# A perceiver layer: x loaded four groups ahead, stage 3 in another order, the gate's product in three fp32r products

## What is computed

```python
x = x + xattn(layernorm(x), ctx)     # cross attention to the 257 context rows, then [hc, hq, hc*hq, hc*bar] @ W_qv + b
x = x + attn(layernorm(x))           # z = layernorm(x); xg = z * sigmoid(z @ Wg.T + bg)
                                     # s = s @ A + xg * Bp; y = s . Cp + Dp * xg, over 32 tokens; layernorm(y + xg) * gamma + beta
x = x + ffn(layernorm(x))            # h = x @ tern(w_fc).T + low rank; relu(h)**2 @ tern(w_proj).T
```

## Time and profile before

| | |
|---|---|
| median of 3 runs | 589.56 us (588.4 to 592.37) |
| the profiled execution | 591.37 us, its span 589.6 us |
| PE busy | 501.3 us (85% of the span) |
| DVE busy | 428.4 us (73%) |
| ACT busy | 363.6 us (62%) |
| POOL busy | 334.3 us (57%) |
| granted clock of TensorE, mean | 0.95 |
| DMA | 69.9 MB, 41.5% of 16 engines' span |

### The profile page before, as it was taken

How to read it: one execution, slowest core, us unless ns; L and a number is a source line. 1 busy time by engine, 2 the same in 40 slices (tenths; PEclk the granted TensorE clock), 3 DMA queues, 4 the chain that set the end, 5 groups by cost and what they waited for, 6 DMA issues and landing times. The chain is left out here.

```text
span 589.6 us, 12951 instructions
## 1 busy us (share of the span) xinstructions
PE 501.3 (85%) x4070; PEld 420.2 (71%) x4070; DVE 428.4 (73%) x1197; ACT 363.6 (62%) x857; POOL 334.3 (57%) x424
## 2 busy tenths in 40 slices
PE   3596999999999999999998716975888988988995
PEld 2375777878787877877786506964777877877884
DVE  2589888888888878887887606943688788788643
ACT  3464767776767766776776405563846846846652
POOL 1488666675757575766665300002767767767653
PEclk9799999999999999999999957995989989989998
DMA  7543365545645475646565761546002202201102
GB/s 225 147 157 100 104 210 156 177 142 175 189 143 176 139 213 131 190 124 205 145 186 149 193 62 39 139 109 148 31 1 72 71 2 73 71 1 36 38 1 71
DMA packets 90035, 69.90 MB, mean 119 GB/s; under 512 B 49504, under 2 KB 73328, under 8 KB 89968
## 3 DMA queue, kind: packets, MB, share of 16 engines
q1 hardware_dynamic: 89968, 69.08, 41.5%
HBM read 55.96 MB, written 13.11 MB: 117 GB/s over the span
## 5 line engine op out<-in xcount | busy, mean ns | idle before, releaser
L1526 POOL TENSOR_TENSOR sq_lo<-scan_x,sq_hi 128x512 fp32r<-128x512 f32 x64 | 83.7, 1308 | 58.5 <-ACT sq_hi L1497 56.5
L1489 ACT ACTIVATE relu<-fc_ps,fc_square 128x512 f32<-128x512 f32 x64 | 43.9, 686 | 54.8 <-PE fc_ps L1438 54.8
L473 PE MATMUL turn_ps<-ident,ctxn 128*128 128x128 f32 x512 | 70.8, 283 | 4.3 <-DMA ctxn<-in_ctx 4.3
L1567 DVE SCALAR_TENSOR_TENSOR scan_x<-fc_ps,relu 128x512 f32<-128x512 f32 x64 | 44.0, 687 | 38.2 <-ACT relu L1489 37.5
L603 ACT COPY ctxT<-turn_ps 128x512 f32<-128x512 f32 x128 | 68.2, 581 | 5.2 <-PE turn_ps L473 5.1
L473 PEld LDWEIGHTS turn_ps<-ident,ctxn 128*128 128x128 f32 x512 | 58.6, 145 | 17.9 <-issue 13.2
L708 POOL TENSOR_TENSOR rstd<-ve,neg_half 128x1 f32<-128x1 f32 x64 | 35.3, 551 | 43.3 <-DVE ve L796 22.5
L722 POOL TENSOR_TENSOR hc_lo<-hc_probT,hc_hi 128x256 fp32r<-128x256 f32 x32 | 23.4, 730 | 56.3 <-ACT hc_hi L610 56.3
L1434 PE MATMUL fc_ps<-toeplitz,fc_T 128*128 128x512 f32 x128 | 54.1, 422 | 0.5 <-DVE scan_x L1567 0.5
L1434 PE MATMUL fc_ps<-xn_lo,fc_T 128*128 128x512 f32 x128 | 53.0, 414 | 0.0
L714 POOL TENSOR_TENSOR proj_in<-proj_in,fc_in 128x512 f32<-128x512 f32 x31 | 49.2, 1588 | 0.0
(11 more groups left out here) (188 smaller groups left out, 1413.3 us busy)
## 6 DMA issues: line engine op xcount, KB each, us to landing
ctxn<-in_ctx SPq DMA_DIRECT2D x32, 1024.0 KB, 5.3
resid<-in_x SPq DMA_DIRECT2D x32, 128.0 KB, 4.7
ctx_end<-in_ctx SPq DMA_DIRECT2D x32, 128.0 KB
gated_tokens<-gated SPq DMA_DIRECT2D x32, 128.0 KB, 5.0
out<-resid SPq DMA_DIRECT2D x8, 512.0 KB, 3.0
scan_x<-gated_tokens SPq DMA_DIRECT2D x60, 64.0 KB, 4.8
scan_tokens<-scan_x SPq DMA_DIRECT2D x4, 768.0 KB, 9.7
y_in<-scan_tokens SPq DMA_DIRECT2D x4, 512.0 KB, 4.4
```

The source lines that it names most:

```text
L473: mm = pe.transpose(turn_ps[b % 2][:, (c * JT + t) * P:(c * JT + t + 1) * P], ctxn[p][:, b, t, c * P:(c + 1) * P], ident[:, :])
L1489: act.activation(relu[m % 2], fc_ps[m % 2][:, :], ACT.Relu, scale=fc_square[:, m:m + 1]).then_inc(relu_done, 1)
L1526: pool.tensor_tensor(sq_lo[:, m, :], sq[m % SQ], sq_hi[:, m, :].bitcast(F32), ALU.subtract).then_inc(sq_lo_done, 1)
L1567: dve.scalar_tensor_tensor(out=sq[m % SQ], in0=fc_ps[m % 2][:, :], scalar=0.0, in1=relu[m % 2], op0=ALU.max, op1=ALU.mult).then_inc(sq_don ...
```

## The change

- x is loaded four groups ahead (AHEAD) with four semaphores; groups 2 and 3 are loaded before the first step.
- The gate's product: ACT's copy makes `zT_hi` in fp32r, DVE takes `zT_lo` after `hcqT`, PE does six fp32r products. `wgT` is split likewise in group 1, where DVE takes `wgT_lo`.
- Stage 3: `low_rank`, `low_rank_hi`, `low_rank_parts` and `split_lo` stand ahead of the tile's other work instead of behind it. y is normalised whole on ACT (`norm_y`, with the deviation as scale), POOL makes its shift, in other places of its order; `add_y` is one addition of 1024 columns behind square 7.
- The end: the last tile's low part is made by DVE (`last_lo`), its product in two halves (`project_last`), and the last chunk is stored in two halves.
- `impulse` lies in a part of `xn` instead of memory of its own.

The diff, cut:

```diff
@@ -261,13 +262,14 @@
 late_loaded = sem("late_loaded")
 states_in = sem("states_in")
-x_loaded = [sem(f"x_loaded{p}") for p in range(2)]
+AHEAD = 4
+x_loaded = [sem(f"x_loaded{p}") for p in range(AHEAD)]
 ctx_loaded = [sem(f"ctx_loaded{p}") for p in range(2)]
 end_loaded = [sem(f"end_loaded{p}") for p in range(2)]
 masks_made = sem("masks_made")
 zeroed = sem("zeroed")
 wg_turned = sem("wg_turned")
-wgT_ready = sem("wgT_ready")
+wgT_hi_ready, wgT_lo_ready = sem("wgT_hi_ready"), sem("wgT_lo_ready")
 ends_turned = sem("ends_turned")
...
@@ -399,9 +401,10 @@
 g, p, has_a, has_b, has_c = stages(base, k)
 inside = not isinstance(g, int)
+if g + AHEAD < GROUPS:
+    at_least(sp, hc_ready, g + 1)
+    load_x(g + AHEAD)
 if inside or g + 2 < GROUPS:
-    at_least(sp, hc_ready, g + 1)
-    load_x(g + 2, p)
     at_least(sp, attended, g + 1)
...
@@ -412,6 +415,8 @@
+for g in range(2, AHEAD):
+    load_x(g)
 for i in range(2):
...
@@ -572,9 +578,12 @@
     mm.then_inc(scored, 1)
 if has_c:
-    at_least(pe, zT_ready, g - 1)
-    for c in range(KD):
-        mm = pe.matmul(gate_ps[:, 0:D], zT[:, c, :], wgT[:, c, :], start=(c == 0), stop=(c == KD - 1))
+    at_least(pe, zT_hi_ready, g - 1)
+    at_least(pe, zT_lo_ready, g - 1)
+    for i, (part, w) in enumerate(((zT_hi, wgT_hi), (zT_hi, wgT_lo), (zT_lo, wgT_hi))):
+        for c in range(KD):
+            mm = pe.matmul(gate_ps[:, 0:D], part[:, c, :], w[:, c, :], start=(i == 0 and c == 0),
+                           stop=(i == 2 and c == KD - 1))
     mm.then_inc(gate_summed, 1)
...
@@ -645,7 +654,9 @@
     at_least(act, z_turned, g - 1)
     at_least(act, gate_summed, g - 2)
-    act.copy(zT[:, :, :], gate_ps[:, 256:256 + D].rearrange("p (k t) -> p k t", k=KD)).then_inc(zT_ready, 1)
+    at_least(act, zT_lo_ready, g - 2)
+    act.copy(zT_hi[:, :, :], gate_ps[:, 256:256 + D].rearrange("p (k t) -> p k t", k=KD)
+             ).then_inc(zT_hi_ready, 1)
 if has_b:
...
@@ -854,7 +865,7 @@
     dve.tensor_scalar(ve2[:, :], mv2[:, 1:2], EPS, None, ALU.add).then_inc(ve2_done, 1)
 if inside or g + 1 < GROUPS:
-    at_least(dve, x_loaded[o], sixteen(base, k, -1))
+    at_least(dve, x_loaded[(g + 1) % AHEAD], 16 * ((g + 1) // AHEAD + 1))
     layer_norm1(g + 1, o, g + 1)
...
@@ -883,8 +894,17 @@
     turned = feat_ps[:, 0:D].rearrange("p (k t) -> p k t", k=KD)
     dve.tensor_tensor(hcqT[:, :, :], turned, hc_probT[o][:, 0, :, :], ALU.mult).then_inc(hcqT_ready, 1)
+if has_c:
+    at_least(dve, zT_hi_ready, g - 1)
+    at_least(dve, gate_summed, g - 2)
+    dve.tensor_tensor(zT_lo[:, :, :], gate_ps[:, 256:256 + D].rearrange("p (k t) -> p k t", k=KD),
+                      zT_hi[:, :, :].bitcast(F32), ALU.subtract).then_inc(zT_lo_ready, 1)
 for s in state_steps[:1]:
     state_sum(s)
+if isinstance(g, int) and g == 1:
+    dve.wait_ge(wgT_hi_ready, 1)
+    dve.tensor_tensor(wgT_lo[:, :, :], gate_ps[:, :].rearrange("p (k e) -> p k e", k=KD),
+                      wgT_hi[:, :, :].bitcast(F32), ALU.subtract).then_inc(wgT_lo_ready, 1)
 if has_b:
...
@@ -995,38 +1016,47 @@
         ins.then_inc(centred, 1)
+def add_first(dve):
+    dve.wait_ge(centred, 2)
+    dve.wait_ge(rstd_y_done, 1)
+    for r in range(CH):
+        ins = dve.scalar_tensor_tensor(out=res(0, r), in0=y_in[:, r, :], scalar=rstd_y[:, r:r + 1],
+                                       in1=res(0, r), op0=ALU.mult, op1=ALU.add)
+    ins.then_inc(x2_done, 1)
 def lower_y(pool, c):
-    pool.wait_ge(mv_y_done, c + 1)
-    at_least(pool, yc_done, 2 * c - 2)
+    pool.wait_ge(rstd_y_done, c + 1)
+    at_least(pool, yn_done, 2 * (c - 1))
     pool.tensor_tensor(neg_mean_y[:, :], mv_y[:, :, 0], minus_one[:, :], ALU.mult).then_inc(neg_mean_y_done, 1)
-def centre_y(act, c, h):
-    act.wait_ge(neg_mean_y_done, c)
+    pool.wait_ge(neg_mean_y_done, c)
+    pool.tensor_tensor(shift_y[:, :], neg_mean_y[:, :], rstd_y[:, :], ALU.mult).then_inc(shift_y_done, 1)
+def norm_y(act, c, h):
+    act.wait_ge(shift_y_done, c)
     for r in half(h):
-        ins = act.activation(y_of(c)[:, r, :], y_of(c)[:, r, :], ACT.Identity, bias=neg_mean_y[:, r:r + 1], scale=1.0)
-    ins.then_inc(yc_done, 1)
+        ins = act.activation(y_of(c)[:, r, :], y_of(c)[:, r, :], ACT.Identity, bias=shift_y[:, r:r + 1],
+                             scale=rstd_y[:, r:r + 1])
+    ins.then_inc(yn_done, 1)
 def times_gamma(pool, c, h):
-    pool.wait_ge(yc_done, 2 * (c - 1) + h + 1)
+    pool.wait_ge(yn_done, 2 * (c - 1) + h + 1)
     part = y_of(c)[:, h * CH // 2:(h + 1) * CH // 2, :]
     pool.tensor_tensor(part, part, gamma_all[:, :].unsqueeze(1).broadcast_to([P, CH // 2, D]), ALU.mult
                        ).then_inc(centred, 1)
-def add_y(dve, c, h):
-    dve.wait_ge(centred, 2 * c + h + 1)
-    dve.wait_ge(rstd_y_done, c + 1)
-    for r in half(h):
-        ins = dve.scalar_tensor_tensor(out=res(c, r), in0=y_of(c)[:, r, :], scalar=rstd_y[:, r:r + 1],
-                                       in1=res(c, r), op0=ALU.mult, op1=ALU.add)
-    ins.then_inc(x2_done, 1)
+def add_y(dve, c):
+    dve.wait_ge(centred, 2 * c + 2)
+    part = resid[:, c * CH:(c + 1) * CH, :]
+    dve.tensor_tensor(part, y_of(c)[:, :, :], part, ALU.add).then_inc(x2_done, 1)
 def x_sums(dve, c):
-    dve.wait_ge(x2_done, 2 * c + 2)
+    dve.wait_ge(x2_done, c + 1)
     at_least(dve, mv_x_done, c)
...
@@ -1062,7 +1092,8 @@
 def deviation_y(pool, c):
     pool.wait_ge(ve_y_done, c + 1)
-    at_least(pool, x2_done, 2 * c)
+    at_least(pool, x2_done, min(c, 1))
+    at_least(pool, yn_done, 2 * (c - 1))
     pool.tensor_tensor(rstd_y[:, :], ve_y[:, :], neg_half[:, 0:CH], ALU.pow).then_inc(rstd_y_done, 1)
...
@@ -1399,11 +1431,17 @@
     if has(c, 2):
         load_y(c + 2)
-    if has(c, -1):
+    if 1 <= c < CHUNKS:
         at_least(sp, out_ready, 2 * c)
         sp.dma_start(out_tok[(c - 1) * TOK:c * TOK, :].rearrange("(r p) d -> p r d", p=P),
                      resid[:, (c - 1) * CH:c * CH, :]).then_inc(out_stored, 16)
-sp.wait_ge(out_stored, 16 * CHUNKS)
+    if c == CHUNKS:
+        for h in range(2):
+            first = (c - 1) * CH + h * CH // 2
+            sp.wait_ge(out_ready, 2 * (c - 1) + h + 1)
+            sp.dma_start(out_tok[first * P:(first + CH // 2) * P, :].rearrange("(r p) d -> p r d", p=P),
+                         resid[:, first:first + CH // 2, :]).then_inc(out_stored, 16)
+sp.wait_ge(out_stored, 16 * (CHUNKS + 1))
...
@@ -1454,16 +1492,31 @@
     mm.then_inc(proj_tile, 1)
+def project_last(c, m):
+    pe.wait_ge(sq_hi_done, tile(c, m) + 1)
+    pe.wait_ge(last_lo_done, 1)
+    for h in range(2):
+        for part in (sq_hi, sq_lo):
+            for r in half(h):
+                mm = pe.matmul(proj_ps[c % 2][h][:, (r % 2) * D:(r % 2 + 1) * D],
+                               part[:, m, r * P:(r + 1) * P], proj_T[:, m, :],
+                               start=False, stop=(part is sq_lo), skip_group_check=True)
+        mm.then_inc(last_half, 1)
 turn_in(0)
 low_rank(0)
 for c in range(CHUNKS + 1):
     for m in range(MT):
+        if m == 7 and has(c, 1):
+            low_rank(c + 1)
         if has(c):
             hidden(c, m)
-        if m == 7 and has(c, 1):
-            low_rank(c + 1)
         if m < BEHIND and has(c, -1):
-            project(c - 1, MT - BEHIND + m)
+            if c == CHUNKS and m == BEHIND - 1:
+                project_last(c - 1, MT - 1)
+            else:
+                project(c - 1, MT - BEHIND + m)
         if m >= BEHIND and has(c):
...
@@ -1498,25 +1551,24 @@
 split_hi(0)
 for h in range(2):
-    centre_y(act, 1, h)
+    norm_y(act, 1, h)
 low_rank_hi(0)
 for c in range(CHUNKS + 1):
     for m in range(MT):
         if m == 5 and has(c, 1):
             split_hi(c + 1)
+        if m == 7 and has(c, 1):
+            low_rank_hi(c + 1)
         if has(c):
             relu_tile(c, m)
-        if m == 7 and has(c, 1):
-            low_rank_hi(c + 1)
         if m >= 1 and has(c):
             square_hi(c, m - 1)
         if m == 0 and has(c, -1):
             square_hi(c - 1, MT - 1)
         if m in (2, 3) and has(c, 1):
             norm_x(act, c + 1, m - 2)
-        if m == 4 and has(c, 2):
-            for h in range(2):
-                centre_y(act, c + 2, h)
+        if m in (4, 5) and has(c, 2):
+            norm_y(act, c + 2, m - 4)
...
@@ -1536,12 +1588,13 @@
     deviation_x(pool, c + 1)
     lower_x(pool, c + 1)
-if m == 3 and has(c, 2):
+if m == 2 and has(c, 2):
+    deviation_y(pool, c + 2)
     lower_y(pool, c + 2)
-    deviation_y(pool, c + 2)
-square_lo(c, m)
-if m in (4, 5) and has(c, 2):
-    times_gamma(pool, c + 2, m - 4)
+if m in (4, 6) and has(c, 2):
+    times_gamma(pool, c + 2, m // 2 - 2)
+if tile(c, m) < CHUNKS * MT - 1:
+    square_lo(c, m)
...
@@ -1571,18 +1624,31 @@
     bank = proj_ps[c % 2][h][:, :].rearrange("p (r d) -> p r d", r=2)
     part = resid[:, c * CH + 2 * h:c * CH + 2 * h + 2, :]
-    at_least(dve, proj_tile, (c + 1) * MT)
+    if c == CHUNKS - 1:
+        dve.wait_ge(last_half, h + 1)
+    else:
```

(23 more changed lines are left out.)

36 lines of the change are left out of this document (20 added, 16 removed).

## The result

| | before | after |
|---|---|---|
| median (4 runs each) | 590.84 us (588.40 to 592.37) | 559.39 us (557.21 to 562.58) |
| ratio | | 0.9476, 95% interval 0.9412 to 0.9540 |
| the profiled execution | 591.37 us, span 589.6 | 562.58 us, span 560.7 |
| PE, DVE, ACT, POOL busy | 501.3, 428.4, 363.6, 334.3 us | 489.6, 426.5, 365.8, 335.6 us |
| start of the 30th L843 (L854 after the change) | 319.93 | 307.50 (-12.4) |

The forecast was 557.6 us, 549 to 570. The lower part of the table splits the 28.9 us by which the two spans differ. In my sum, x, the gate and `wgT_lo` gave 12.4 us for the first stretch, pauses and clock 18.0 for the third, and the tail 1.6. The second stretch had no term.

The account below looks back on a forecast made before the run. Stage 1 was bound by a DVE, ACT and POOL loop plus late x, stage 3 by PE's pauses for lr_parts. 11.3 + 1.4 - 0.3 + 12.5 + 5.5 + 1.6 = 32.0 us off the 589.56 median gave 557.6, range 549 to 570.

Parts of the forecast that it names:

- x four groups ahead: Stage 1: DVE's waits for x all go and long groups become short ones, 11.3 us gained.
- the gate: Stage 1: fp32r products save PE 0.26 us per group, 0.05 arrives in 28 groups, 1.4 us gained.
- `wgT_lo`: Group 1 of stage 1: made once, it holds up DVE; 0.3 us lost, bound 1.6.
- pauses: Stage 3: PE's six waits for lr_parts, 2.28 us each, shrink to 0.2 each, 12.5 us gained.
- clock: Stage 3: four low-clock stretches of 1.38 us go with the pauses, 5.5 us gained.
- the tail: Kernel's end: DVE's results finish earlier and the last store is smaller, 1.6 us gained, bounds 0.5 and 2.5.
- Rival B: Stage 1: PE is the real bound and the gate's saving arrives, 8 instead of 1.4 us, 551; chance 0.12.
- Rival C: Stage 1: zT_lo isn't hidden, 10 us lost and the gate's gain missing, 570 us; chance 0.08.
- E: Stage 1: slower, as a shorter gate product lets TensorE's clock fall to 1.2 GHz, groups up to 18 us; chance 0.02.
- three moves that I counted: Stage 3: low_rank before tile 7, its ACT and DVE parts before relu and square 7, add_y after square 7.
- `add_y`: Stage 3: one 1024-column addition of 1.38 us after waiting 1.3 us for POOL, against 2.91 + 0.87 us before.
- Rival A: Stage 3: the pause only shrinks, DVE's addition slowed proportionally to 4.6 us; 9.6 us, 567; chance 0.12.

Follow-up runs that it names:

- experiment 3: Changed kernel with the gate's product as before (plain fp32, no zT_lo, no wgT_lo): 559.41 us, ratio 0.9489 to the kernel before.
- experiment 4: Changed kernel with zT_lo computed twice per group on DVE: 566.61 us; changed kernel with a fourth partial gate product on PE: 561.82 us.
- experiment 6: Changed kernel with add_y ahead of square 7: 567.52 us; changed kernel with low_rank and its parts behind tile 7's work again: 558.15 us.
- experiment 5: Changed kernel with POOL's state product before beta and DVE's state sum before zT_lo: 575.13 us; with hcwT's first half ahead of z too: 573.12 us.
- the repeat: The changed kernel run once more, unaltered, for a second profile: 558.31 us, ratio 0.9441 to the kernel before.

## Why the prediction was right, point by point

**x four groups ahead, 11.3 us.** Right in cause and size: the 30th L843 comes 10.9 us earlier with x alone, the run 12.0 +- 2.8 us, and the order of SP's queue was shown to be the cause.

**The gate, 1.4 us.** The size came about right by luck: misreadings made up for each other. First, I took 8 pairs of fp32r products at 0.233 us off the 2.83 us and gave the remaining 0.96 to the old gate, and 3 x 0.233 = 0.70 to the new one. But the first pair behind another kind of product costs more than 0.233. Before, `project`'s first pair behind the fp32 gate takes 0.42 us to the next one; now the gate's first pair, behind the scores, takes 0.34 (211.48 to 211.82). With that the products save some 0.15 us a group and not 0.26, an estimate from the 2.88 and 2.78 us of experiment 3 and the hold. That hold for `hq_lo`, 0.05 us, is the one that I had allowed for, so 0.10 are left. Second, I let only 0.10 arrive because I took DVE's queue for the chain that closes a group. PE's closes it, and what PE is quicker arrives (experiment 4). Third, 0.05 is lost again to the wider spacing that came with the stage-3 part (experiment 3), which no term had. So 0.06 us a group were seen, and 0.05 were said. Rival B named the right bound, but its 8 us rested on the same 0.26. `zT_lo` was hidden as said, and its price without cover measured 0.27 us a group (0.33 said). Rival C falls. So does E: the clock of stage 1 is 1.00 with PE busy 189.0 of 190 us.

**`wgT_lo`, 0.3 us.** The first L854 came 0.6 us later (35.59 against 34.96): in the bounds, twice the value. `hq_lo` came 1.9 us later (1.6 said), and `prob` then took 0.36 us instead of 1.66, since POOL's memset was nearly over.

**The pauses, 12.5 us, and the clock, 5.5.** All six pauses went, and the clock is full in stage 3 from 403.6 on. Of the three moves that I counted, `add_y`'s was enough; the two that bring `low_rank` forward weren't needed (experiment 6). That the low stretches come from the pauses is inferred: they follow them, and they are gone without them. Their number, four, is partly chance, since the kernel with x alone has three behind the same six pauses. The 1.4 us to spare measured 1.48. Two terms were mis-sized. A pause cost 21.64 - 19.08 = 2.56 us a chunk and not its 2.28 of waiting: 0.10 us of the difference lie in the tile behind it (2.22 us against 2.12), the rest in the one that holds it. And the 0.2 us that I left at the turn of `xn` did not come. Together (0.28 + 0.2) x 6 = 2.9 of the 3.2 us between 18.0 and 21.2.

**`add_y`.** I gave it 1.3 us of waiting for POOL and 1.38 of its own; it took 2.30. POOL's instruction ended 1.21 us after DVE's start, and 1.09 more followed. The Trainium skill, "SBUF — State Buffer", section "Who interferes with whom", says that the one that issues second is blocked for the other's whole instruction. The traces here agree in three places: `add_y` (1.21 us until POOL's end, then 1.09 for 1024 columns), `last_lo` (0.47, then 0.55 for 512), and `hc` in experiment 5, which ended 0.15 us after POOL's product. In these three POOL's instruction started first. In the ordinary groups of the changed kernel `hc` is recorded 0.01 to 0.07 us ahead of POOL's addition of beta and still ends 0.15 us after it, so the order isn't borne out there. Rival A, which slows the addition in proportion to 4.6 us, falls.

**The tail, 1.6 us.** It brought 1.4. `last_lo` took 1.02 us and not 0.6: POOL's last `sq_lo` was under way for 0.47 us when it started.

**What had no term.** From the 30th L843 to the first low-rank product it was 89.5 us in the profile of before, and 95.6 in that of after. In the other profiles it was 90.2 to 91.9 us eight times, 92.7 to 93.8 three times, and 98.2 in that of the gate alone. The changed kernel itself had 90.4 in its other profile, and two kernels with the very same code in this stretch had 90.9 (experiment 4) and 93.6 (experiment 6). So most of it varies from one execution to the next. It is the better part of why the profiled execution is 3.2 us above the median. The traces show where it lies. From the 30th L854 to the first product with a Toeplitz block it is 42.6 us in the profile after, 38.8 in the repeat and 37.6 before. No engine computes there from 340 to 350 us of the profile after, and the DMA share is 0.57. The first products then ran at 1.2 GHz for 5.7 us and not 2.6, which goes with another 1.4 us; what follows takes 46.4 to 46.8 us in every kernel. Why the stretch ahead of the products is longer in some executions stays open.

## What to carry to other kernels

When an engine waits for a load, look first at what stands ahead of it in the DMA queue: here an order without cost cured the same waits as a deeper prefetch. When two chains close a loop within 0.1 us of each other, a saving on one of them is worth at most the distance to the other, and adding work to each in turn measures that distance better than arithmetic on a timeline. Price a change of product type by the distance from the product ahead of it to the one behind it, since in these traces the change from one kind to the other has a price of its own.

## What the runs showed that I had not expected

- DVE's `hc` (one tensor and two scalars per partition, 128x256) takes 0.76 to 0.96 us beside POOL's addition of beta and 1.50 us when POOL's product of 1.54 us starts just ahead of it. In both cases it ends some 0.15 us after POOL's instruction. Where that ended 0.23 us after `hc`'s start, in one group of the kernel with eight gate products, `hc` took 0.41 us. Where a POOL instruction stands decides what a DVE instruction costs here, and the order with the product 0.7 us earlier was 16 us slower.
- In the kernels with x early, three periods of stage 1 are 0.35 us longer: 9.42 with x alone, eight groups apart, and 9.35 to 9.38 in the changed kernel, five and thirteen groups apart. In two of them the changed kernel shows 0.28 to 0.31 us in which DVE waited for nothing that the profile knows, always at the same groups (89.24 and 135.50 us; 89.01 and 135.27 in the repeat). With late x this was covered. The cause wasn't looked for.
- The distance between fp32r pairs of 256 columns is 0.233 to 0.234 us in the kernels without the stage-3 part and 0.239 to 0.240 in all with it, though in stage 1 these differ from the others only by one small tile in the layout. Whether the tile does it wasn't tried.
